# A top-1 mixture-of-experts layer on one core: one 512-wide gather per tile, b2 seeded into PSUM by ScalarE, and W1 of a tile copied within SBUF by DMA into three buffers

## The reference, cut to what matters

```python
# x (2, 1024, 256), 8 experts, H = 1024, D = 256; all float32
w_bot = einsum('bg,got->bot', cond_8, weight * mask)      # per batch element
xf    = einsum('bnt,bot->bno', x, w_bot) + bias           # 2048 rows of 256
top1  = argmax(xf @ gate_w.T + gate_b)                    # an expert for each row
for e in range(8):
    h = relu(xf @ w1[e].T + b1[e]); y = h @ w2[e].T + b2[e]
    out += where(top1 == e, y, 0)
return x + out
```

## Time and profile before

| | |
|---|---|
| time, median of 3 runs | 200.39 us (199.42 to 200.75) |
| the profiled execution's own time | 199.18 us |
| its span | 197.5 us |
| PE busy | 159.0 us (81% of the span) |
| DVE busy | 131.1 us (66%) |
| POOL busy | 121.5 us (62%) |
| ACT busy | 102.1 us (52%) |

### The profile page before, as it was taken

How to read it: one execution, slowest core, us unless ns; L and a number is a source line. 1 busy time by engine, 2 the same in 40 slices (tenths; PEclk the granted TensorE clock), 3 DMA queues, 4 the chain that set the end, 5 groups by cost and what they waited for, 6 DMA issues and landing times.

```text
span 197.5 us, 6297 instructions
## 1 busy us (share of the span) xinstructions
PE 159.0 (81%) x1768; PEld 135.2 (68%) x1769; DVE 131.1 (66%) x228; ACT 102.1 (52%) x167; POOL 121.5 (62%) x115
## 2 busy tenths in 40 slices
PE   0085999928959999999994995999999999997500
PEld 0025758814459999999883885999999998986400
DVE  0499398998589999997859737887653444533100
ACT  0700865870087879888692575775554454421000
POOL 1293599902732998386575647888787677255930
PEclk9999999985979999999999799999999999999975
DMA  4999920840497777767766772011212221111110
GB/s 111 364 413 411 404 85 4 277 149 0 120 362 294 243 221 220 235 215 228 223 223 228 225 223 79 28 56 54 77 52 69 72 71 45 32 56 43 44 58 0
DMA packets 12025, 31.16 MB, mean 158 GB/s; under 512 B 2903, under 2 KB 5079, under 8 KB 11872
## 3 DMA queue, kind: packets, MB, share of 16 engines
q1 hardware_dynamic: 8272, 24.39, 35.5%
q0 software_dynamic: 3024, 6.30, 10.5%
q10 hardware_dynamic: 704, 0.17, 0.4%
HBM read 27.96 MB, written 4.85 MB: 166 GB/s over the span
## 4 chain that ended last, share of the span: by engine, by line
DMA 33%; issue 23%; POOL 14%; DVE 10%; PE 8%; POOLq 5%; SPq 1%; DVEq 0%
DMA out<-res,tok_of_slot 23%; POOL xg L425 5%; DMA b_all<-b 4%; POOL res L437 4%; DVE stage L587 4%; DMA wsp<-cond_w 3%; POOLq L435 3%; POOL out L442 3%; POOL res L431 2%; PE psum L805 2%; PE psum L834 2%; DMA xg<-xf_rows,tok_of_slot 1%; DMA res<-x_rows,tok_of_slot 1%; PE psum L883 1%; PE psum L821 1%
## 5 line engine op out<-in xcount | busy, mean ns | idle before, releaser
L931 PE MATMUL psum<-wsp,hT 128*128 x504 | 59.9, 277 | 6.5 <-DVE hT L742 6.0
L914 PE MATMUL psum<-xs,stage 128*128 128x128 f16 x1008 | 61.4, 222 | 2.2 <-DVE xs L734 2.2
L914 PEld LDWEIGHTS psum<-xs,stage 128*128 128x128 f16 x1008 | 59.4, 99 | 3.4 <-issue 3.0
L931 PEld LDWEIGHTS psum<-wsp,hT 128*128 128x128 f16 x504 | 48.1, 99 | 14.4 <-issue 8.1
L431 POOL DMA_INDIRECT res<-x_rows,tok_of_slot x21 | 25.5, 1213 | 29.9 <-DMA out<-res,tok_of_slot 26.5
L425 POOL DMA_INDIRECT xg<-xf_rows,tok_of_slot x21 | 29.9, 1426 | 20.9 <-issue 12.1
L538 ACT ACTIVATE psum<-b_col 128x1024 f32 x21 | 21.5, 1022 | 26.0 <-DVE hT L742 14.3
L632 DVE SCALAR_TENSOR_TENSOR wsp<-wsp x25 | 31.3, 1289 | 4.2 <-issue 4.2
L742 DVE SCALAR_TENSOR_TENSOR hT<-psum,hT 128x512 f16<-128x512 f32 x42 | 26.9, 682 | 9.3 <-issue 9.3
L519 ACT ACTIVATE wsp<-wsp x25 | 25.3, 1051 | 5.2 <-issue 2.5
L442 POOL DMA_INDIRECT out<-res,tok_of_slot x21 | 23.2, 1104 | 3.8 <-issue 3.5
(11 more groups left out here) (111 smaller groups left out, 124.6 us busy)
## 6 DMA issues: line engine op xcount, KB each, us to landing
wsp<-w_all SPq DMA_DIRECT2D x32, 512.0 KB, 5.2
wsp<-cond_w SPq DMA_DIRECT2D x4, 512.0 KB, 7.1
wsp<-x_t SPq DMA_DIRECT2D x2, 1024.0 KB, 11.0
b_all<-b SPq DMA_DIRECT2D x1, 1024.0 KB, 8.2
xf_rows<-stage SPq DMA_DIRECT2D x1, 768.0 KB, 3.7
xf_rows<-stage SPq DMA_DIRECT2D x1, 640.0 KB, 3.3
xf_rows<-stage SPq DMA_DIRECT2D x1, 384.0 KB, 3.0
xg<-xf_rows,tok_of_slot POOLq DMA_INDIRECT x21, 3.7
```

The lines of the kernel that those rows point to most:

```text
L914: last = t_.matmul(o, w1s[:, b, w:w + P], xs[:, b, xp, k * P:(k + 1) * P], start=False, stop=(c % 4 == 3 and k == KD - 1 and wp == 1), ski ...
L931: last = t_.matmul(ps_y[b], hT[:, b, hp, c * P:(c + 1) * P], w, start=(c == 0 and w is high and hp == 0), stop=(c == KH - 1 and w is low))
```

## The change

`x` and `xf` stand side by side in one HBM tensor of 512-wide rows, `both_rows`: SP stores `xf` into its left half, and ACT's list issues one copy of `x`, HBM to HBM, into its right half, ahead of its first weight chunk. One gather per tile brings both halves into `rows_in` (RING = 6 buffers, four gathers ahead of the loop). POOL no longer adds b2. ACT writes b2 times 4096 into the PSUM bank of `y` (`seed_y`), and layer 2 accumulates onto it. W1 of tile i+2 is copied by a DMA that ACT's list issues in round i, from SBUF to SBUF, into one of three buffers. It is left out where tile i-1 has the same expert. DVE still copies W1 for tiles 0 and 1. With the experts of these inputs DVE's copies go from 11 to 2, and 12 DMAs of 1 MB are issued: for tiles 2, 5 to 11, 14 to 16 and 20.

```diff
-RING = 4
+RING = 6
+W1_BUFS = 3
+GATHERED = 4
...
-            def gather_x(i):
-                if i >= RING:
-                    pool.wait_ge(xT_ps, i - RING + 1)
-                g.indirect_dma_start(xg[:, i % RING, :], None, xf_rows, token(i),
-                                     bounds_check=TOK - 1, oob_is_err=False).then_inc(x_in[i % RING], 16)
-
-            def gather_res(i):
+            def gather(i):
                 if i >= RING:
                     pool.wait_ge(stored[i % RING], 16 * (i // RING))
-                g.indirect_dma_start(res[:, i % RING, :], None, x_rows, token(i),
-                                     bounds_check=TOK - 1, oob_is_err=False).then_inc(res_in[i % RING], 16)
-
-            def add_b2(i):
-                e = pool.value_load(tile_expert[0:1, i:i + 1], min_val=0, max_val=E - 1)
-                pool.wait_ge(res_in[i % RING], 16 * (i // RING + 1))
-                g.tensor_tensor(res[:, i % RING, :], res[:, i % RING, :],
-                                b2_all[:, bass.ds(e, 1), :].rearrange("p a n -> p (a n)"), ALU.add).then_inc(res_ready, 1)
+                g.indirect_dma_start(rows_in[:, i % RING, :], None, both_rows, token(i),
+                                     bounds_check=TOK - 1, oob_is_err=False).then_inc(x_in[i % RING], 16)
...
-            for i in range(RING):
-                gather_x(i)
-            gather_res(0)
-            pool.wait_ge(ld_b2, 16)
+            pool.wait_ge(x_stored, 16)
+            for i in range(GATHERED):
+                gather(i)
             pool.wait_ge(experts_known, 1)
             used = load_used(pool)
-            for i in range(SLOT_TILES + 2):
-                if_used(pool, used, i + RING, lambda: gather_x(i + RING))
-                if_used(pool, used, i + 1, lambda: gather_res(i + 1))
-                if_used(pool, used, i, lambda: add_b2(i))
-                if i >= 2:
-                    if_used(pool, used, i - 2, lambda: scatter(i - 2))
+            for i in range(SLOT_TILES):
+                if_used(pool, used, i + GATHERED, lambda: gather(i + GATHERED))
+                if_used(pool, used, i, lambda: scatter(i))
...
             w_t_out(1)
+            act.dma_start(both_rows[:, D:2 * D].rearrange("(t p) d -> p t d", p=P),
+                          x_rows.rearrange("(t p) d -> p t d", p=P)).then_inc(x_stored, 16)
             high(0)
...
+            def seed_y(i, b, e):
+
+                if late(i, 2):
+                    act.wait_ge(y_ready, i - 1)
+                a.mul(ps_y[b], b2_all[:, bass.ds(e, 1), :].rearrange("p a n -> p (a n)"),
+                      WSCALE * WSCALE).then_inc(y_seeded, 1)
...
+            def w1_load(i, r, turn, plan):
+
+                act.wait_ge(lo_late, plan.goal + AHEAD)
+                if late(i, W1_BUFS):
+                    act.wait_ge(h_ps, 2 * i - 4)
+                with act.If(plan.next_same == 0):
+                    act.dma_start(w1s[:, r % W1_BUFS, :],
+                                  wsp[:, bass.ds(plan.next_expert * (CPE * 2 * CH), CPL * 2 * CH)]).then_inc(w1_in[r % W1_BUFS], 16)
+                with act.Else():
+                    act.sem_inc(w1_in[r % W1_BUFS], 16)
...
                 if_used(act, used, i, lambda: h_hi(i, b))
+                if_used(act, used, i + 2, lambda: w1_load(i + 2, (r + 2) % RING, turn + (1 if r >= RING - 2 else 0), next_plan))
+                if not late(i, 1):
+                    act.wait_ge(ld_b2, 16)
+                if_used(act, used, i, lambda: seed_y(i, b, plan.expert))
...
             def y_out(i, b, r):
                 dve.wait_ge(y_ps, i + 1)
-                dve.wait_ge(res_ready, i + 1)
...
             def tile(i, b, r, turn, plan):
-                if_used(dve, used, i + 1, lambda: w1_copy(i + 1, 1 - b, plan))
+                if not late(i, 1):
+                    w1_copy(1, plan)
                 if_used(dve, used, i + 1, lambda: x_lo(i + 1, 1 - b))
...
-            def layer1(i, b):
-                pe.wait_ge(w1_ready, i + 1)
+            def layer1(i, b, r, turn):
+
+                if late(i, 2):
+                    pe.wait_ge(w1_in[r % W1_BUFS], 32 * turn - (32 if r < 2 else 16 if r < 5 else 0))
+                else:
+                    pe.wait_ge(w1_ready, i + 1)
                 pe.wait_ge(xlo_ready, i + 1)
                 pe.wait_ge(h_seeded, i + 1)
...
-                if late(i, 2):
-                    pe.wait_ge(y_ready, i - 1)
+                pe.wait_ge(y_seeded, i + 1)
```

More of the change, by code:

```diff
@@ L216, in build @@
         primed = sem("primed")
+        y_seeded = sem("y_seeded")
         h_seeded = sem("h_seeded")
@@ L245, in build @@
         w1_ready = sem("w1_ready")
+        w1_in = [sem(f"w1_in{n}") for n in range(W1_BUFS)]
         h_ps = sem("h_ps")
@@ L931, in layer2 @@
                         last = t_.matmul(ps_y[b], hT[:, b, hp, c * P:(c + 1) * P], w,
-                                         start=(c == 0 and w is high and hp == 0), stop=(c == KH - 1 and w is low))
+                                         start=False, stop=(c == KH - 1 and w is low), skip_group_check=True)
                 last.then_inc(y_ps, 1)
```

44 lines of the change are left out of this document (17 added, 27 removed).

## The result

The changed kernel takes **208.8 us** in the median (207.14 to 210.46), beside 199.9 us for the kernel before (197.25 to 200.75) on the same chip. That is 1.05 times as long, with an interval of 1.032 to 1.068. Forecast were 197.0 us, in a range that ended at 205. The profiled execution took 208.57 us and its span is 206.8, against 199.18 and 197.5 before.

The account below looks back on a forecast made before the run. The bound was a chain of scatter, gather, b2, `y_out`, splits, `h_lo`, layer 2, with the weight stream barely ahead. Tile 11 +2.6, tiles 12 to 20 -1.2, end -4.1 gave -2.7 us: 197.0 us, range 188.5 to 205.

Parts of the forecast that it names:

- The step that failed: ACT: ACT's load rounds: branch, issue and `seed_y` add 1.64 us (0.4 to 2.0), giving 6.5 us against PE's 5.53.
- The load's landing: W1 load from issue to landing: 6.3 us, between bounds of 4.4 and 8.2.
- my own rival: A W1 load takes 8.2 us, so tile 11 starts at 134.6; total 204 us, chance 0.12.
- The pace of 6.5 us a tile: Tiles 5 to 11: each tile follows the last by ACT's 6.5 us, with tile 11 at 127.4.
- Tile 2's start: Layer 1 of tile 2: load issued at 63.35 lands at 69.7, PE idles 2.8 us; tile 3 starts 4.0 late.
- The lower clock: After PE's idle stretch at tile 2, part of the work runs at 1.2 GHz, costing 1.2 us more.
- The stream: Weight chunk stream: each W1 load sets it back 1.5 us (0.6 to 2.7); it just keeps up, at no cost.
- that rival: The weight stream starves: loads take their full 2.7 us from it, +7.9 us, total 205; chance 0.22.
- The gain over tiles 12 to 20: Tiles 12 to 20, no stream: nine tiles at 5.53 us take 49.8 instead of 51.0, 1.2 us gained.
- The end: Last tile's layer 1 to the last scatter's issue: 9.3 us instead of 13.4, 4.1 us gained.
- The copy of `x`: HBM copy of 2 MB before the first gathers: has 22 us, hidden by 8 us or so.
- POOL and DVE: Both off the path: POOL loses its second gather, b2 sum and landing wait; DVE loses nine 1.2 us W1 copies.

Follow-up runs that it names:

- written out: The changed kernel with ACT's rounds 2 to 13 written out instead of looped: 200.5 us, and 199.5 us (1.003 times the kernel before) when run again.
- without W1 DMA: The changed kernel with W1 copied by DVE into two buffers as before, not by DMA: 192.72 us, on another chip 192.24 us, 0.969 times the kernel before.
- the best version: The changed kernel with DVE copying W1 into two buffers instead of the DMA: 192.72 us, then 192.24 us, 0.969 times the kernel before.

## Why the prediction was wrong, step by step

| start of layer 1 | forecast | after | written out | without W1 DMA |
|---|---|---|---|---|
| tile 2 | 69.7 | 69.87 | 71.50 | 68.08 |
| tile 5 | 88.4 | 90.07 | 91.23 | 85.20 |
| tile 8 | 107.9 | 109.16 | 110.21 | 102.68 |
| tile 9 | 114.4 | 122.61 | 116.37 | 109.50 |
| tile 11 | 127.4 | 137.73 | 128.79 | 123.10 |
| tile 20 | 177.2 | 189.38 | 180.11 | 173.93 |

- **The step that failed: ACT.** "A load round adds a branch, an issue and `seed_y`" priced what the round executes, 1.64 us. It did not ask what the longer code does to the loop, and so the sum has nothing for the jump back, which took 6.8 us against 0.3 before. Against the forecast the trace is 1.3 us late at tile 8, 8.2 at tile 9 and 11.3 at tile 10 (due at 120.9): PE idled 6.71, its layer 1 then took 1.70 longer, and the load issued behind the jump was late by 1.72. That is 10 of the 12.2 us by which tile 20 is late, and with it of the whole miss (208.8 for 197.0). No rival had it, so the range missed as well.
- **The load's landing was too short.** Forecast 6.3, from 4.4 to 8.2. Measured 7.15 and 8.46 in the chain after, 7.37 and 8.85 written out; only the load of tile 2 was short in the first trace (see there). I took the middle on the ground that the stream lies beside the load and not ahead of it. The trace has it ahead: the nearest row was the b2 load of the earlier trace rows, with two chunks in front of it. By 8.2 my own rival gave 204.
- **The pace of 6.5 us a tile was right in number** (6.2 to 6.5 from tile 5 to tile 8), but not shown to be ACT's: without `seed_y` it stayed, with ACT waiting.
- **Tile 2's start was right in number** (69.87 and 75.99 for tiles 2 and 3; forecast 69.7 and 76.5), but by luck. The load was issued at 64.36, not 63.35, and landed in at most 5.5 us, not 6.3. Layer 1 waited 1.05 us for it and not some 3, since PE had already stood 1.03 us for `seed_y`, which ACT reaches only behind the load's wait for DVE (the row below). The lower clock that was forecast behind this wait did not come: the next layer 2 took 2.79 us. Written out, the load took 7.37 and layer 1 waited 3.30, as described.

```profile
65.80 2.79 PE L936 MATMUL psum<-wsp,hT 128*128 x24 [1.03 <-ACT psum L533]
```

- **The stream held.** SP's 22 issues took 66.5 us from 58.47 instead of 58.8: 7.8 us, or 1.0 for each of the eight loads up to tile 11, not 1.5. ACT's chunks never waited for it by microseconds, and that rival fell.
- **The gain over tiles 12 to 20 did not come.** Nine tiles took 51.65 us, not 49.8; written out 51.3, before 51.0. PE is busy for 41.1 us of the 42 from 148 to 190: there was no slack of POOL's chain to take, and the last three steps between tiles are 5.8 to 5.9 us long, where I had put the floor of 5.53.
- **The end was right in number:** from the last layer 1 to the end of the span 17.4 us instead of 21.7, 4.3 gained; forecast 4.1. But the forecast had all of it ahead of the last scatter's issue, 9.3 us after the last layer 1. It is issued after 10.9 (before 13.4), which gains 2.4; the other 1.8 lie behind the issue (6.5 us to the end of the span instead of 8.3) and were not in the sum:

```profile
200.32 0.98 POOL L432 DMA_INDIRECT out<-rows_in,tok_of_slot  x1 [2.89 <-DVE rows_in L749]
```

- **The copy of `x` was hidden,** as said: issued at 25.11, landed in 8.4 us, and the first tile starts 0.5 later than before.
- **POOL and DVE** are off the path, as said. But most of what that is worth was reached by six buffers alone.

## What to carry to other kernels

Where a change adds instructions to a loop, look at the loop's own jump: at its length and its place in the engine's list, and at what is queued in the DMA engines when it is taken. A big transfer issued just ahead of the jump is, as it seems here, paid for by the jump. Write the rounds out; shifting the loop took the stall away as well, but the time came back in one job of two. And a copy within SBUF that an engine with slack does in 1.2 us isn't improved by a DMA of 2.5 us of all sixteen engines, in a kernel whose DMA engines are 0.72 busy: price it as the sum of shares, not as what is idle. Change the cheapest part alone first; here two more buffers held 4 of the 6 us that the best version gained.

## What the runs showed of the hardware

- A jump back over ACT's loop of 297 instructions took 6.8 us from the branch to the loop's top behind a 1 MB load, 4.9 behind half of one; over 391 instructions in a kernel without such loads, 3.0. Over 302 instructions that stood 32 earlier in the list, or 297 that stood 83 later, it took 0.3.
- Two large plain transfers of two issuers were served one behind the other: 95% for one queue, at most 5% for the other, for some 2 us.
- Single register loads became slower beside the loads within SBUF; in the version without the W1 DMA the longest of ACT's takes 302 ns. ACT's reads of the plan, in the kernel after and then before (duration in ns, shortest, median, longest):

```profile
L272 ACTq TENSOR_LOAD <-tile_plan x27: 273/298/1427, 50.5 to 193.5; - x27
```

```profile
L269 ACTq TENSOR_LOAD <-tile_plan x28: 273/278/293, 50.6 to 179.0; - x28
```

- A gather of 128 rows of 2 KB took 8.0 us to land beside the weight stream, and the copy of 2 MB within HBM 8.4 us with little beside it. A copy of 1 MB within SBUF by DMA landed in 6.6 to 8.9 us beside the stream, and once in 5.5; DVE did the same copy in 1.25 us.
